# Cross-attention with a routed feed-forward on Trainium2: row writes in pairs, copies moved, and a prologue that splits two weights late

## The reference

```python
# x: (16, 256, 256), ctx: (16, 77, 192); 16 heads of 64; the last 4 context tokens are prompt (IPA) tokens
xn = layernorm(x)
q  = xn @ Wq + lora(xn, q)                 # lora(t, j) = t @ down_j @ up_j * alpha_j / 32, rank 32
k, v = org @ Wk + lora(org, k), org @ Wv + lora(org, v)        # org: the first 73 context tokens
out = attention(q, k, v) + attention(q, ipa @ Wk_ipa, ipa @ Wv_ipa)
x = x + out @ Wo + bo + lora(out, o)
xn = layernorm(x)
combine = softmax over the top 2 of 8 experts of xn @ gate_w
x = x + sum over experts of combine_e * (silu(xn @ w1_e) @ w2_e)
```

## Time and profile before

| | |
|---|---|
| median of three runs | 832.87 us |
| the profiled execution | 830.35 us, its span 828.6 us |
| TensorE busy | 695.4 us (84%) |
| VectorE, ScalarE, POOL busy | 528.4 (64%), 449.2 (54%), 494.1 us (60%) |
| mean granted clock of TensorE | 0.963 |
| DMA | 54.69 MB, mean 66 GB/s |

### The profile page before, as it was taken

The page is one execution under the profiler, slowest core; times in us unless marked ns, Lnnn a source line. Parts: engine busy times, 40 slices in busy tenths (PEclk is TensorE's granted clock), DMA queues, the critical chain, the costliest instruction groups (busy, mean ns, idle before and its releaser), DMA issues.

```text
span 828.6 us, 23021 instructions
## 1 busy us (share of the span) xinstructions
PE 695.4 (84%) x7980; PEld 580.9 (70%) x7981; DVE 528.4 (64%) x1226; ACT 449.2 (54%) x772; POOL 494.1 (60%) x584
## 2 busy tenths in 40 slices
PE   6757889799788789789799898864499999999994
PEld 2235777677677677677677776643398888888894
DVE  5955786686586586586586586573255555555552
ACT  1537775674675675675674675661244343443441
POOL 2227467667667667667668668666147555655565
PEclk9999999999999999999999999987599999999998
DMA  9901001101101101101101101101535556555450
GB/s 267 285 1 40 28 18 61 52 14 64 52 13 64 52 13 64 52 13 64 52 13 65 52 13 64 53 13 62 161 66 98 81 89 98 86 91 81 83 91 6
DMA packets 41676, 54.69 MB, mean 66 GB/s; under 512 B 6320, under 2 KB 36016, under 8 KB 41648
## 3 DMA queue, kind: packets, MB, share of 16 engines
q1 hardware_dynamic: 26176, 35.90, 14.8%
q0 software_dynamic: 14384, 17.33, 12.0%
q10 hardware_dynamic: 1088, 1.08, 0.4%
HBM read 30.36 MB, written 25.76 MB: 68 GB/s over the span
## 4 chain that ended last, share of the span: by engine, by line
PE 57%; ACT 14%; issue 13%; DVE 8%; DMA 2%; POOL 2%; SPq 1%; another core or an unknown queue 1%; POOLq 1%; ACTq 0%; DVEq 0%
PE ps L1321 46%; PE ps L1382 5%; ACT pt_s L873 4%; PE ps L1392 2%; ACT wstage L992 2%; ACT xn L935 2%; PE ps L439 2%; DVE ot_s L1073 2%; DMA out_x<-pt_s,token_of 1%; POOL out_x L413 1%; PE ps L1347 1%; ACT ot_s L873 1%; DVE picked L1227 1%; DVE prob L1114 1%; ACT row_words L944 1%
## 5 line engine op out<-in xcount | busy, mean ns | idle before, releaser
L413 POOL DMA_INDIRECT out_x<-pt_s,token_of x78 | 125.9, 1615 | 31.1 <-issue 30.2
L492 ACT ACTIVATE q_s<-ps 128x512 f32<-128x512 f32 x78 | 46.6, 597 | 132.6 <-PE ps L1321 132.1
L1321 PE MATMUL ps<-q_s,ffnw 128*128 128x256 f16 x936 | 110.0, 275 | 0.0
L1321 PE MATMUL ps<-ffnw,ot_s 128*128 x936 | 108.7, 273 | 0.1
L565 DVE TENSOR_TENSOR ot_s<-q_s,ot_s 128x512 f16<-128x512 f32 x78 | 54.0, 692 | 85.8 <-ACT ot_s L496 57.8
L1144 DVE TENSOR_REDUCE mx<-prob 128x16 f32<-128x1168 f32 x64 | 47.9, 790 | 95.3 <-ACT prob L913 90.9
L1321 PEld LDWEIGHTS ps<-ffnw,ot_s 128*128 128x128 f16 x936 | 90.2, 98 | 13.3 <-issue 1.9
L1321 PE MATMUL ps<-wo_s,ot_s 128*128 128x256 f16 x768 | 93.8, 281 | 5.4 <-DVE ot_s L1073 4.4
L1321 PEld LDWEIGHTS ps<-q_s,ffnw 128*128 x936 | 90.7, 99 | 10.7 <-issue 0.2
L731 POOL TENSOR_TENSOR prob<-prob,mx 128x1168 f32<-128x1168 f32 x64 | 77.6, 1235 | 31.0 <-DVE mx L1144 30.7
L1321 PE MATMUL ps<-xt_s,wq_s 128*128 128x256 f16 x768 | 89.0, 277 | 3.8 <-DVE xt_s L1073 1.9
(11 more groups left out here) (179 smaller groups left out, 1311.9 us busy)
## 6 DMA issues: line engine op xcount, KB each, us to landing
prob<-rows_dram SPq DMA_DIRECT2D x39, 264.0 KB
wstage<-in_ffn_w SPq DMA_DIRECT2D x16, 512.0 KB
x_sb<-in_x SPq DMA_DIRECT2D x4, 1024.0 KB, 11.8
out_x<-x_sb SPq DMA_DIRECT2D x16, 256.0 KB, 2.2
out_x<-pt_s,token_of POOLq DMA_INDIRECT x78
rows_dram<-wstage ACTq DMA_DIRECT2D x4, 264.0 KB
rows_dram<-wstage SPq DMA_DIRECT2D x4, 264.0 KB
pt_s<-in_wq SPq DMA_DIRECT2D x2, 512.0 KB, 4.4
```

The costliest lines, as they stand in the source:

```text
L413: pool.indirect_dma_start(out_rows, bass.IndirectOffsetOnAxis(ap=token_of[:, j % UNROLL, c:c + 1], axis=0), y_sb[:, j % UNROLL, c, :], Non ...
L492: act.activation(h32[:, half, :], h_ps(j, half), ACT.Silu, scale=1 / WSCALE).then_inc(silu_done, 1)
L1321: last = pe.matmul(o, lhs(a, n), rhs(c, n), start=(i == 0), stop=(i == len(steps) - 1))
```

## The change

It has two halves. **In the loop:** POOL's row writes of batch b-2 now go out in body b, two before `shift(b, 0)` and two behind it; ScalarE's FFN copies (`fw_high`) move from before the head copies to between the two score copies; POOL's low part of the FFN block and the bias add move ahead of `row_low`; VectorE's residual moves behind query block 1 and also aggregates statistics of batch b+2, which `next_stats` takes in the same body; `place_rows` moves ahead of head block 1 and gets a wait for the rows of the batch before; `x2n` gets memory of its own. SP loads the next FFN block once the present one is split. **In the prologue:** six tiles of `x` are loaded first, two more later, the rest in three loads behind the splits of `Wv`, `Wv_ipa` and `Wo`, which are staged in `x_sb`. The factors lie in two groups of partitions (0 to 31 and 64 to 95), `up` is loaded twice, and a pair of products runs before each wait. Layer statistics are for six tiles, with POOL's power in place of the square root. The splits of `Wv` and `Wv_ipa`, the prompt values and the factor products of `Wo` move into batch 0, the split of `Wo` and `project(0, .)` into batch 1. The low parts of the context and of `Wv_ipa` are POOL's, that of `Wk_ipa` and `Wo` VectorE's. The hardware loop runs 2 to 13 on ScalarE and VectorE, 2 to 14 on TensorE.

The diff, cut to its core:

```diff
+LEAD = 3 * TPB
...
-        stage = [pt_stage[:, 0, :], pt_stage[:, 1, :], prob_flat[:, 12 * TILES:12 * TILES + 2048],
-                 q_s[:].rearrange("p a m n -> p (a m n)").bitcast(F32)]
+        stage = [pt_stage[:, 0, :], pt_stage[:, 1, :], prob_flat[:, 0:2048],
+                 x_stage[:, 1, :], x_stage[:, 2, :], x_stage[:, 3, :]]
...
-        x2n = xn
+        x2n = sb("x2n", [P, TPB, DM], F32)
...
             load_lora(0, q_down_t, q_up, q_alpha)
             load_job(0)
             load_lora(1, k_down_t, k_up, k_alpha)
+            load_x(0, LEAD, x_in)
             load_job(1)
             load_lora(2, v_down_t, v_up, v_alpha)
...
+            load_job(3)
+            load_job(4)
+            load_lora(3, o_down_t, o_up, o_alpha)
+            load_job(5)
...
+            sp.dma_start(wstage[:], ffn_w[0]).then_inc(fw_in, 16)
+            load_x(LEAD, 8, x_more)
...
# POOL
+            def body(b):
+                if settled:
+                    scatter(b - 2)
+                if first:
+                    vipa_low(0)
                 shift(b, 0)
+                if first:
+                    vipa_low(1).then_inc(w_split_p, 1)
+                if settled:
+                    scatter_pick(1)
                 shift(b, 1)
                 normalise(b, 0)
                 if not first:
                     rstd_2(b - 1)
                 normalise(b, 1)
-                if not first:
-                    row_low(b - 1)
+                pool.wait_ge(fw_hi, b + 1)
+                pool.tensor_tensor(fw[1], wstage[:], fw[0], ALU.subtract).then_inc(fw_split, 1)
...
-                    scatter(b - 1)
-                    scatter_pick(1)
...
# ScalarE
                 copy_scores(b, 0)
                 if not last:
                     xt(b + 1)
+                if second:
+                    split_job(5)
+                if not (first or second):
+                    fw_high(b)
                 copy_scores(b, 1)
+                if first:
+                    split_job(3)
                 exp(b, 0)
+                if first:
+                    normalise_lead(2)
...
+                if first or second:
+                    fw_high(b)
                 exp(b, 1)
...
                 v(b, 0)
                 if first:
+                    ipa_v_hi(act)
...
-                act.wait_ge(fw_in, 16 * b + 16)
-                act.activation(wstage[:], wstage[:], ACT.Copy, scale=WSCALE).then_inc(fw_scaled, 1)
...
# VectorE
+            def next_stats(b):
+                for t in range(TPB):
+                    dve.bn_stats(st2[:, TPB + t, :], x_sb[:, bass.ds(tile, 1), :].rearrange("p t d -> p (t d)"))
...
                 maxima(b, 0)
                 if not last:
                     xt(b + 1)
+                if x_left:
+                    next_stats(b + 2)
+                if second:
+                    job_lo(5)
                 maxima(b, 1)
+                if first:
+                    job_lo(3)
                 sums(b, 0)
                 if not last:
                     q(b + 1, 0)
-                if not first:
-                    residual(b - 1)
                     q(b + 1, 1)
+                if not (first or second):
+                    residual(b - 1, x_left)
                 sums(b, 1)
...
                 ot(b, 0)
-                ot(b, 1)
                 if not first:
                     place_rows(b - 1, chain)
+                ot(b, 1)
+                if first:
+                    job_add(5, 0)
                 ot(b, 2)
                 ot(b, 3)
+                if first:
+                    for step in range(1, 4):
+                        job_add(5, step)
...
+                dve.wait_ge(scattered, 64 * b + 16)          # in place_rows
...
# TensorE
+            def lora_pair(j, step):
+                for g in (0, 1):
...
+                        last = pe.matmul(lora_bank(j, step, g)[0:rows, :], downs(j, g),
+                                         ups(j, g)[:, step * 512:step * 512 + 512], start=True, stop=True)
...
+                if second:
+                    pe.wait_ge(w_split, 5)
+                    project(b - 1, 0)
+                    project(b - 1, 1)
                 if first:
-                    pe.wait_ge(w_split, 3)
+                    pe.wait_ge(w_split, 4)
                 new_values(b, 0)
+                if first:
+                    values_ipa()
...
+                if first:
+                    lora_pair("o", 1)
+                    for step in (2, 3):
+                        pe.wait_ge(lora_add, 5 + step)
+                        lora_pair("o", step)
+                    pe.wait_ge(lora_add, 10)
```

More of the change, by code:

```diff
@@ L168, in build @@
         vipa_dram = nc.dram_tensor("vipa_dram", (BATCH, IPA, 2, ID), F16, kind="Internal").ap()
-        x_in = [sem(f"x_in{c}") for c in range(4)]
+        x_in = sem("x_in")
+        x_more = sem("x_more")
+        x_rest = sem("x_rest")
         lora_in = [sem(f"lora_in_{j}") for j in "qkvo"]
@@ L174, in build @@
         ctx_in = [sem(f"ctx_in{k}") for k in range(2)]
-        pst_in = [sem(f"pst_in{s}") for s in range(4)]
+        pst_in = [sem(f"pst_in{s}") for s in range(6)]
         consts = sem("consts")
@@ L953, in gap_e, with body @@
                 act.activation(gap_exp[:], gap[:], ACT.Exp).then_inc(gap_expd, 1)
-            def body(b, first, last, x_left):
+            def body(b, last, x_left):
+                first, second = (isinstance(b, int) and b == n for n in (0, 1))
                 copy_scores(b, 0)
@@ L1104, in _, with zero_rows @@
             dve.memset(gap[:], 0.0).then_inc(row_lo, 1)
-            for w in (wk_s, wv_s, kipaw, vipaw, ctx_s):
-                for part in (0, 1):
-                    last = dve.memset(w[CDR:P, part, 1, :].bitcast(F32), 0.0)
-            last.then_inc(rows_zeroed, 1)
-            def bn(first, count):
-                for t in range(first, first + count):
-                    if t % 8 == 0:
-                        dve.wait_ge(x_in[t // 8], 16)
-                    dve.bn_stats(stats[:, t, :], x_sb[:, t, :]).then_inc(st_done, 1)
+            def zero_rows(weights):
+                for w in weights:
+                    for part in (0, 1):
+                        last = dve.memset(w[CDR:P, part, 1, :].bitcast(F32), 0.0)
+                last.then_inc(rows_zeroed, 1)
             def xt(b):
@@ L1181, in residual @@
                 dve.memset(hold[:], 0.0)
-                for t in range(TPB):
+                for t in range(2 * TPB if x_left else TPB):
                     last = dve.bn_aggr(ln2[:, t, :], st2[:, t, :])
@@ L1232, in place_rows, with body @@
                 assert c.n == ROUTE, c.n
-            def body(b, first, last):
+            def next_stats(b):
+                dve.wait_ge(x_more, 16)
+                if not isinstance(b, int):
+                    dve.wait_ge(x_rest, 48)
+                for t in range(TPB):
+                    tile = b * TPB + t
+                    dve.bn_stats(st2[:, TPB + t, :], x_sb[:, bass.ds(tile, 1), :].rearrange("p t d -> p (t d)"))
+            def body(b, last, x_left):
+                first, second = (isinstance(b, int) and b == n for n in (0, 1))
                 maxima(b, 0)
@@ L1478, in rank, with body @@
                 last.then_inc(rank_mm, 1)
-            def body(b, first, last):
+            def body(b, last):
+                first, second = (isinstance(b, int) and b == n for n in (0, 1))
                 if not first:
@@ L1511, in body @@
                 transpose_probs(b, 3)
+                if first:
+                    pe.wait_ge(ipa_split, 4)
+                if second:
+                    pe.wait_ge(x1_done, b)
                 if not last:
```

453 lines of the change are left out of this document (237 added, 216 removed).

## The result

Four executions of the changed kernel took 782.64 to 786.86 us, median **785.61 us**, against 831.75 us in the same comparison: a ratio of 0.944 (95% interval 0.940 to 0.947). The forecast was 764.1, its range 750 to 799. The forecast gain was 66 us; 46 came between the medians, 43.5 between the two profiled executions (830.35 and 786.86 us), which are what the forecast's sum goes by.

What follows compares the result with a forecast made beforehand. Prologue waits and TensorE's 14% loop idling were what could be won. Gains of 49.7 (loop), 16.4 (prologue, batch 0) and 1.0 (batch 15), less 0.9 (batch 1), took 830.35 to 764.1 us; own range 750 to 778, full 750 to 799.

Steps and rivals of the forecast that it cites:

- the stall: TensorE's second scores in the loop: 2.5 us of holes beside POOL's four row writes, forecast 0 with writes in pairs.
- the wait for the row numbers: End of each loop batch: TensorE's wait for `slot_i`, forecast to fall from 2.3 to 0.3 us.
- rival A: Loop: the stall stays, bound to the place behind the loop's head, not to four writes; 797.6 us, chance 0.14.
- rival B: Loop: softmax late, one late link of 1 to 1.5 us a batch; 781.6 us, chance 0.10.
- The wait at the second value product: Loop: new TensorE wait of 1.0 us, as the residual ahead of the second sums delays the third query block's split.
- The copies' cover of 0.1 us: Loop: ScalarE's FFN copies end at 5.0 us, just before the second scores end at 5.1, so they cost nothing.
- First scores at 39: Prologue: first scores start at 39 us instead of 70.3.
- Batch 0 at 37.5: Batch 0: 22.5 us plus 14.0 of moved-in work, 1 for clock; batch 1 starts at 76.5 instead of 92.85.
- Batch 1 at 31.7: Batch 1: split of `wo` and its late projection make it 31.7 us against 30.8, 0.9 lost.
- C: Loop: slower, each pair starves TensorE as four writes did, decided by over 2.65 us a pair; 838 us, chance 0.05.

## Why the prediction was right, and where not

The direction and the two waits that were to go (the stall and the wait for the row numbers) came as forecast. The size came only in part: 785.6 us lies in the full range because that range was drawn out to rival A's price, and it is 21 us from the forecast and 4 from rival B's 781.6, which had a chance of 0.10. Term by term:

- **The stall** (0 for both pairs): right in outcome. The ground I gave, that a pair is over before the 3.2 us are up, was wrong: a pair beside the second scores costs 1.05 us, one at the first scores 1.3, with the first hole 0.85 us after the write began. The place saved it: the first write starts 0.05 to 0.22 us before the first scores end. The forecast had that time right (0.9 us), but didn't rest on it.
- **The wait for the row numbers** (2.3 to 0.3): right, it is 0. I kept 0.15 us a batch for the clock, and it was full (1.00 over 121.47 to 486.86). What the sum didn't have is that a wait left standing can bring the lower clock and cost more than itself. Where only one of the two parts was in the kernel, sums of this kind came out 22 to 25 us too good (797 against 818.56, 798 against 822.85).
- **The wait at the second value product** (1.0): 0.74, and gone when the split is moved ahead of the second sums, so the reason given for it holds.
- **The picks**: the step that failed in the loop. I moved POOL's low part of the rows in the text without asking what VectorE does beside it: 0.63 us a batch.
- **The copies' cover of 0.1 us** (rival B): the cover failed, not by the copies but because the first score copy starts up to 1.87 us late beside a row write. That is 0.85 us in each of 8 batches, about 7 of the 9.9 us that the loop missed. Rival B's end was right for those batches, its cause was not. The rest of the 9.9 is 13 times 0.63 for the picks, less 0.26 that the wait at the value product fell short and 0.15 for the clock.
- **First scores at 39**: 47.5. The layer statistics took POOL 3.9 us (18.72 to 22.6) and not 1.3; 2.08 of it is its first operation, on 6 elements a partition, which ends 0.06 us after VectorE's low part of `wq` (18.48 to 20.74). It looks like the same hold-up as at the picks, with POOL second this time; no run tried it apart. The context landed at 19.2, not 17. And the first factor pair of `Wv` (3.96 us) ran ahead of the queries, which I had left out: they started at 28.77 instead of 21.8. These 7 us are most of the 8.5; the prologue is where the forecast missed most for its size, 7.0 won and not 16.4.
- **Batch 0 at 37.5** (36.5 and 1 for the clock): 38.3, near, but by luck. The low part of `Wv` took 5.83 us beside POOL's low part of `Wv_ipa` and its second subtraction, where I had 2.35 for such a pair, and TensorE waited 6.61 us at the fourth query block, where the kernel before waited 1.88 and I had added 2.0. So the other terms together were some 2 us too dear; which of them, the runs don't tell apart.
- **Batch 1 at 31.7**: 35.6. I charged the split of `Wo` and its projection, not that the low part stands ahead of the second maxima and so holds the query banks: a 3.58 us wait, with a clock share of 0.91 over the batch. Moving the low part takes that wait away (1.54 us left in one kernel, none in the other), but TensorE then waits 2.5 us at the late projection, and batch 1 took 33.25 us (clock share 1.00) and 34.92 (0.85) against 34.84 (0.90) unmoved. So most of what batch 1 cost isn't pinned to that place.

The chances: the forecast's mechanism held, its own range (750 to 778) didn't; A falls by the undone pairs, and C's point, 2.65 us a pair, isn't reached beside the second scores (1.05) or at the first (1.3). C's terms, for that matter, add up to 839 us and not 838.

## What to carry to other kernels

Before an operation of POOL is moved, look up what VectorE runs at its new time, and the other way round; where both read two SBUF operands, charge the wait to whoever comes second, as VectorE's comparison paid here, and POOL's first operation on the statistics seems to have. When a wait of TensorE in a loop is removed or left, sum up with the granted clock: two edits that win little alone can win much together. Place indirect writes where TensorE has long matmuls (its query products took 5.40 us beside four writes as without), and behind the copies that start a chain.

## What was not expected of the hardware

- A row write issued by POOL holds up other engines: TensorE's scores (48 matmuls and as many weight loads in 1.03 us) by 1.05 to 1.3 us (two writes) to over 2 us (four), not its query products; ScalarE's first copy by 0.5 to 1.87 us. Through what, no run shows.
- The delays don't depend on a loop branch on ScalarE: written out, they are the same to 0.05 us.
- In two kernels a wait of 2.1 to 2.4 us for the row numbers was followed by a granted clock near 0.5 (1.2 GHz, where the full level is 2.4) for some 3.5 us in 12 of 13 batches. The same came behind other idle time of TensorE: behind the wait of 2.1 us for the probabilities (12 batches), the stall of four writes (8), and the wait of 1.38 us for the router's input (10). In the changed kernel, with waits of at most 0.85 us in batches 2 to 14, the loop ran at 1.00.
